# Deformable sampling in batches of four groups instead of three, with the per-image work placed anew

## The reference

```python
x = x + deformable_conv(group_norm(x))        # 3x3, offsets and masks from a convolution of its own
t = x.reshape(4, 256, 64)
t = t + attention_block(layer_norm(t))        # 8 heads of 32, then a gated feed-forward, two layer norms
t = t + recurrence(layer_norm(t))             # 256 steps: i, g, o gates; c = h*c + i*g; h = o*tanh(c)
```

## Time and profile before

| what | us |
|---|---|
| median of 3 runs | 383.69 |
| lowest, highest | 382.93, 396.51 |
| the profiled execution | 384.46 |
| its span, first to last instruction | 382.6 |

### The profile page before, as it was taken

The page is one execution under the profiler, slowest core; times in us unless marked ns, Lnnn a source line. Parts: engine busy times, 40 slices in busy tenths (PEclk is TensorE's granted clock), DMA queues, the critical chain, the costliest instruction groups (busy, mean ns, idle before and its releaser), DMA issues.

```text
span 382.6 us, 15322 instructions
## 1 busy us (share of the span) xinstructions
PE 352.9 (92%) x5878; PEld 193.0 (50%) x5931; DVE 238.8 (62%) x1230; ACT 224.6 (59%) x1072; POOL 56.6 (15%) x124
## 2 busy tenths in 40 slices
PE   7998999989999999999899999998999999988886
PEld 2566675554564455455545554554455454543332
DVE  3487775646666666666666566656675666664443
ACT  1476764616854775477558655864686478544342
POOL 3101001311211220122012111211121112110000
PEclk9999999999999999999999999999999999999999
DMA  7000000000000000000000000000000000000000
GB/s 230 3 1 4 12 15 17 14 2 3 3 3 2 9 2 4 3 5 4 3 3 7 5 2 6 2 4 3 7 3 4 3 5 5 2 2 6 2 3 6
DMA packets 4807, 3.98 MB, mean 10 GB/s; under 512 B 3837, under 2 KB 4286, under 8 KB 4734
## 3 DMA queue, kind: packets, MB, share of 16 engines
q1 hardware_dynamic: 4432, 2.45, 2.4%
q10 hardware_dynamic: 302, 0.55, 0.5%
HBM read 2.20 MB, written 0.26 MB: 6 GB/s over the span
## 4 chain that ended last, share of the span: by engine, by line
PE 64%; DVE 15%; ACT 12%; issue 7%; DMA 1%; POOL 0%; DVEq 0%; ACTq 0%; POOLq 0%
PE bank L790 18%; PE bank L399 9%; PE bank L570 8%; DVE bank L1340 6%; PE bank L586 5%; DVE H L1350 5%; PE bank L485 5%; ACT bank L975 4%; ACT bank L968 4%; PE bank L473 4%; PE bank L607 4%; ACT E L894 2%; PE bank L687 1%; PE bank L721 1%; PE bank L422 1%
## 5 line engine op out<-in xcount | busy, mean ns | idle before, releaser
L399 PE MATMUL bank<-FB 128*128 128x512 bf16 (+3 forms) x430 | 126.1, 364 | 9.0 <-issue 7.8
L790 PEld LDWEIGHTS bank<-H,VW 64*32 64x32 f32 x3060 | 52.1, 106 | 104.9 <-DVE H L1350 103.1
L968 ACT ACTIVATE bank<-bank 64x8 f32<-64x8 f32 x256 | 37.6, 147 | 87.7 <-PE bank L790 84.8
L790 PE MATMUL bank<-H,VW 64*32 64x4 f32 x3060 | 74.3, 176 | 12.1 <-DVE H L1350 1.9
L1340 DVE TENSOR_TENSOR_SCAN bank<-bank,SU 64x12 f32<-64x12 f32 x256 | 48.5, 190 | 49.8 <-ACT bank L968 47.1
L1350 DVE SCALAR_TENSOR_TENSOR H<-TO,bank 64x4 f32<-64x4 f32 x256 | 40.7, 159 | 44.8 <-ACT bank L975 34.1
L376 POOL TENSOR_SCALAR E<-E,rinv 128x256 f32<-128x256 f32 x62 | 29.8, 482 | 125.8 <-DVE rinv L1138 125.8
L399 PEld LDWEIGHTS bank<-FB 128*128 128x128 bf16 x483 | 37.8, 98 | 20.7 <-issue 3.1
L975 ACT ACTIVATE bank<-bank 64x4 f32<-64x4 f32 x256 | 38.4, 150 | 16.0
L972 ACT ACTIVATE TO<-bank 64x4 f32<-64x4 f32 x256 | 43.8, 171 | 6.2
L1334 DVE SCALAR_TENSOR_TENSOR SU<-H,bank 64x4 f32<-64x4 f32 x256 | 41.3, 161 | 9.1
(11 more groups left out here) (122 smaller groups left out, 310.6 us busy)
## 6 DMA issues: line engine op xcount, KB each, us to landing
AW<-in_attn_w SPq DMA_DIRECT2D x1, 768.5 KB, 7.9
DW<-in_dcn_w SPq DMA_DIRECT2D x1, 288.0 KB, 6.3
X<-in_x_fm SPq DMA_DIRECT2D x1, 256.0 KB, 3.7
X<-in_x_fm ACTq DMA_DIRECT2D x1, 256.0 KB, 6.1
T<-T0T SPq DMA_DIRECT2D x16, 16.0 KB, 1.8
Y<-YT SPq DMA_DIRECT2D x16, 16.0 KB, 1.8
out_dram<-OUT SPq DMA_DIRECT2D x8, 32.0 KB, 1.5
K<-in_consts ACTq DMA_DIRECT2D x1, 181.0 KB, 4.0
```

Of the source, the lines that this page charges most:

```text
L399: nc.tensor.matmul(idle[:, 0:n], FB[:, 0:P], FB[:, 0:n], start=True, stop=True)
L790: mm = nc.tensor.matmul(gate_out(m, gate, r, slice(B * s, B * (s + 1))), VW[0:C, gate, r], H[0:C, (STEPS * m + s - 1) % RING, :], start=Fa ...
L968: nc.scalar.activation(GT[:, :, 1:3].rearrange("p b g -> p g b"), b_cell[m % 2][0:C, 0:2 * P].rearrange("p (g s b) -> p g s b", g=2, b=B)[ ...
```

## The change

- `BATCH` goes from 3 to 4, and with it the slots of A and AT from 6 to 8; there are 9 batches.
- On TensorE `channels` and `values` of a batch move ahead of its gathers, `keys_queries` behind them, and the batches in which they stand change. `channels(0)` stood behind the gathers of batch 5 (groups 12 to 14) and stands behind turns 20 to 23.
- On VectorE `sampled(0)` stood behind A14 and stands behind A22; `token_stats(0)` stood behind A16 and stands behind A26; `token_norm(0)` stood behind A18 and stands behind A27; `first_queries` stands two batches behind its keys. For image 2 all of them come behind the last A.
- On ScalarE z_out(3) is ahead of AT 0, z_out(6) ahead of AT 16, and the hats of image 1 stand behind AT 4. `masks(1)` comes at group 7.
- z(6) writes to banks 7 and 3 and waits for z_out(5); z(7) waits for z_out(6).
- The fills of the head have 5632 and 2560 columns.

```diff
-BATCH = 3
-TOKENS_AT = (4, 7, 10)
-CHANNELS_AT = (5, 8, 11)
-KEYS_AT = (6, 9)
-VALUES_AT = (6, 9)
+BATCH = 4
+TOKENS_AT = (4, 6, 8)
+CHANNELS_AT = (5, 7)
+KEYS_AT = (5, 7)
+VALUES_AT = (6, 8)
-COLS_LOAD = 4608
-COLS_GROUPS = 2048
+COLS_LOAD = 5632
+COLS_GROUPS = 2560
...
-        b_z = [(banks[i], banks[j]) for i, j in ((3, 4), (5, 6), (0, 1), (3, 4), (5, 3), (6, 7), (5, 3), (6, 7))]
+        b_z = [(banks[i], banks[j]) for i, j in ((3, 4), (5, 6), (0, 1), (3, 4), (5, 3), (6, 7), (7, 3), (6, 7))]
...
-                    pe.wait_ge(z_sb, 2 * (i - 1))
+                    pe.wait_ge(z_sb, 2 * i)
...
-                    pe.wait_ge(z_sb, (8, 14, 16, 16)[b])
+                    pe.wait_ge(z_sb, (8, 10, 16, 16)[b])
...
                 if j in TOKENS_AT:
                     tokens(TOKENS_AT.index(j))
-                if j in KEYS_AT:
-                    keys_queries(KEYS_AT.index(j))
+                if j in CHANNELS_AT:
+                    channels(CHANNELS_AT.index(j))
+                if j in VALUES_AT:
+                    values(VALUES_AT.index(j))
                 if j == 1:
                     offsets_turned(1)
                 if j >= 1:
                     for g in range(BATCH * (j - 1), BATCH * j):
                         gather(g)
+                if j in KEYS_AT:
+                    keys_queries(KEYS_AT.index(j))
                 if 1 <= j <= 4:
                     z(3 + j)
-                if j in CHANNELS_AT[:-1]:
-                    channels(CHANNELS_AT.index(j))
-                if j in VALUES_AT:
-                    values(VALUES_AT.index(j))
...
-            z_out(2, 0)
-            z_out(2, 1)
+            for i in (2, 3):
+                for h in range(2):
+                    z_out(i, h)
...
             for g, (b, k) in enumerate(GROUPS):
-                if k == HATS_AT and b + 1 < B:
+                if g == 4 * BATCH:
+                    z_out(6, 0)
+                    z_out(6, 1)
+                if k == HATS_AT and 1 <= b < B - 1:
                     hats_abs(b + 1, slice(0, TAPS), b + 3)
-                if k == HATS_AT + 2 and b + 1 < B:
+                if k == HATS_AT + 2 and 1 <= b < B - 1:
                     hats_relu(b + 1, slice(0, TAPS), b + 3)
...
-                if j == 0 and g < 2:
-                    z_out(3, g)
-                elif 2 <= j <= 5 and g % BATCH < 2:
+                if j in (2, 3, 5) and g % BATCH < 2:
                     z_out(2 + j, g % BATCH)
+                if g == BATCH:
+                    hats_abs(1, slice(0, TAPS), 3)
+                    hats_relu(1, slice(0, TAPS), 3)
...
-                elif g == 2 * SOONER:
+                elif g == 2 * BATCH:
                     positions(1)
-                elif g == TAPS:
+                elif g == 3 * BATCH:
                     mask_scaled(1)
...
-                if last == BATCH - 1 and j - 1 in KEYS_AT:
-                    first_queries(KEYS_AT.index(j - 1))
-                if last == BATCH - 1 and j in TOKENS_AT:
-                    sampled(TOKENS_AT.index(j))
-                if last == 1 and j in CHANNELS_AT:
-                    token_stats(CHANNELS_AT.index(j))
-                if last == 0 and j - 2 in TOKENS_AT:
+                if last == 2 and j - 1 in TOKENS_AT:
+                    sampled(TOKENS_AT.index(j - 1))
+                if last == 2 and j - 2 in TOKENS_AT:
+                    token_stats(TOKENS_AT.index(j - 2))
+                if last == 3 and j - 2 in TOKENS_AT:
                     token_norm(TOKENS_AT.index(j - 2))
+                if last == 3 and j - 2 in KEYS_AT:
+                    first_queries(KEYS_AT.index(j - 2))
```

More of the change, by code:

```diff
@@ L930, in _ @@
                         values_out(VALUES_AT.index(j))
+            channels_out(2)
             keys_out(2)
@@ L1184, in heads_of @@
                                              src[:, 0:HG * P].rearrange("p (g b t) -> p g t b", g=HG, b=B)[:, :, :, images])
+            sampled(2)
+            first_queries(1)
+            token_stats(2)
             token_norm(2)
```

## The result

The changed kernel takes 388.89 us (median of 6 runs), the kernel before beside it 383.21; the ratio of the means is 1.0157, with a 95% interval of 1.0133 to 1.0182. (Now and then an execution of any of these kernels takes 3% longer, one of the 6 of the kernel before 396.51; ratios and medians from here on leave such executions out.) It is slower, by 5.7 us, and stays within the two per cent. The profiled execution has a span of 386.8 us.

The account below looks back on a forecast made before the run. TensorE, busy 92% of the span, was taken as the bound; sampling +5.4, fills -1.7 and clock +2.0 gave +5.7, so 390.2 for the profiled execution, less 0.77 for the median: 389.4 us, range 386.0 to 393.0.

Parts of the forecast that it names:

- batches of four: Sampling on TensorE: nine batches in place of twelve save changes between turns and gathers, -0.9 us.
- first batches: Start of the sampling: VectorE must make eight As instead of six before the first gather, +0.7 us, between 0.3 and 1.2.
- `tokens(0)`: Sampling: TensorE waits 1.8 us, as VectorE's masked(2) waits for ScalarE's hats_relu(2); +0.8 us against before.
- `channels(0)`: Behind turns 20 to 23: TensorE waits for YT, behind masked(3) and ScalarE's hats_relu(3); +4.0 us, bounds nothing and 4.4.
- keys: keys_queries(0) and (1) behind the gathers: the next turns wait for late ATs, twice, +0.8 us, between 0.3 and 1.2.
- clock in the wait: The 4.0 us wait before channels(0) drops TensorE's clock to 1.2 GHz for a stretch, +2.0 us, ends 0 and 4.0.
- fills: Head: added fills keep TensorE working, so its clock rises before the first offsets convolution, -1.7 us.
- Rival D: At channels(0): masked(3) finds its hats done, both new waits go, not slower, 381.6 us; chance 0.10.

Follow-up runs that it names:

- the run with fills in the wait: The changed kernel with twelve fills of 512 columns put on TensorE ahead of channels(0); 387.66 us, ratio to the kernel before 1.0132.
- the kernel with both hats early: The changed kernel with ScalarE's hats of image 2 ahead of AT 12, of image 3 ahead of AT 18; 381.77 us, ratio 0.9972.

## Why the prediction was right

The forecast of 389.4 with 386.0 to 393.0 held (388.89), and so did the mechanism, but for the way in which the fills work and two sizes. Step by step, measured between the starts of what TensorE does:

| step | forecast | measured |
|---|---|---|
| batches of four | -0.9 | -1.0 |
| first batches | +0.7 | +0.8 |
| `tokens(0)` | +0.8 | +0.7 |
| `channels(0)` | +4.0 | +3.9 |
| keys | +0.8 | +0.9 |
| clock in the wait | +2.0 | +1.4 in the profile, +1.2 by medians |
| fills | -1.7 | -2.0 in the profile, -1.0 by medians |

The first six rows add up to 6.7, and from the first turn to the last `tokens` the trace is 6.7 us longer (52.38 against 45.67).

- *Batches.* Nine of 1.89 and 1.88 against twelve of 1.46 and 1.45: 0.5 each for turns and gathers.
- *First batches.* The first eight turns take 5.21 us where two full batches are 3.78, the third batch 2.34 instead of 1.89: 1.9 of waits, against 1.1 in the first six turns before.
- *tokens(0).* The wait was put at 1.8 and is 1.49, 0.5 more than before; with 0.2 for the later arrival it makes 0.7. hats_relu ends 31.14 + 0.72 - 28.91 = 2.95 us after turn 12 begins, to the hundredth as read from the earlier trace rows; `tokens(0)` comes 8.09 after it, 8.15 was said. TensorE arrives 0.2 later than reckoned, as turns 15 and 19 each wait a little for an AT; those waits had been put at nothing.
- *channels(0).* hats_relu ends 4.01 us after turn 20 begins (4.07 said), `channels(0)` comes at 5.80 (5.87).
- *Keys.* Two batches of 2.34 and 2.33 against 1.89.
- *The clock in the wait.* It fell in the 3.75 us and not in the 1.49, as reckoned, but the price was taken from the whole first convolution, and the stretch at the lower clock was shorter: gathers 3.03 - 1.88 and channels 0.61 - 0.37, against the run with fills in the wait.
- *Fills.* The clock was up before the convolution, as said, but not by the road that was given: TensorE doesn't work without a gap, as the second fills run at the higher level, end early and leave 1.29 us. The size was off too. The 2.0 of the profiled execution was read right (4.37 to 2.35); the step that failed was to take that execution as the rule for its head. Of the 29 runs of the kernel before only 2 took longer than its 384.46, and by the medians half of the gain was there already. The forecast took both the 1.7 and the 0.77 by which this execution lies above the median, though its late clock is part of the reason for the 0.77.

The two last errors, 0.8 and 0.7 by the medians, have opposite signs, which is why the sum came out closer than its terms; that is luck. The forecast's own range of 388 to 391 doesn't follow from the bounds of its terms, which are wider (0 to 4.0 for the clock alone). (The two spans differ by 4.2 us only: x took 3.7 us to land in the profile before and 3.0 in the one after, and nothing in the change touches its load.) Rival D named the point that decides: with the hats done in time the forecast was 381.6, and the kernel with both hats early took 381.77. The case against D, the order in the code, was what the experiments moved.

Of the two sentences from the Trainium skill, the one on idle gaps ("TensorE: Matmul & The Clock Gate", section "Why this matters for your kernels") agrees with the trace: the 3.75 us wait brought the clock down, the 1.49 didn't. The one on transposes (same page, "Part 4: PE-mode transpose") was not tested: what runs while the clock comes back here are gathers.

## What to carry to other kernels

A deeper ring lets an engine run ahead only as far as the last thing it needs from an engine that doesn't; before giving a consumer more slots, follow each of its inputs back and see at which of the other engine's steps it is made. Here three activations of 0.7 us had to move by a few places, and the same rings turned from 1.6% slower to 0.3% faster, as much as the fills alone give. Read the gain of a warm clock from several executions: one profile may hold the rare case, as here, where 2 of 29 runs were as long.

## What the runs showed of the hardware

- A TensorE wait of 3.75 us took the clock to the lower level (PEclk 1.00 up to 45 us, 0.57 from 45 to 49, with the wait's end at 45.63), and 2.6 us of fills inside it kept it at 1.00. Waits of 0.99 and 1.49 us left it alone.
- Whether the higher level is reached before the first convolution differs between executions of the same head: with nine and four fills the convolution took 4.37 us in the profile of the kernel before and 2.35 in that of the changed kernel with the old fills.
- A matmul batch cut in two costs: three gathers and one take 1.52 + 0.58 us in one place and 1.45 + 0.59 in another, four together 1.88.
